# The end of the second mixture: DVE's order of the routed rows and the last two residuals

## What is computed

```python
x = x + tanh(g_ffn[1]) * ffn(layernorm(x))
# ffn, with 8 experts of width 176, two for each token, and a shared part of width 352:
shared = silu(x @ Ws_gate) * (x @ Ws_up) @ Ws_down
scores = softmax(x @ W_router);  topk_vals, topk_idx = top_k(scores, 2)
h = silu(einsum('td,edh->eth', x, We_gate)) * einsum('td,edh->eth', x, We_up)
routed = einsum('etd,te->td', einsum('eth,ehd->etd', h, We_down), combine)
return routed + shared
```

## Time and profile before

| | us |
|---|---|
| median of 3 runs | 683.2 |
| all runs | 682.86, 683.20, 689.97 |
| profiled execution | 675.47 |
| its span | 673.7 |

### The profile page before, as it was taken

One profiled execution on the slowest core, in us unless ns is written; L12 is line 12 of the kernel. 1 busy time (PEld: TensorE's weight loads), 2 busy tenths in 40 slices (PEclk: granted clock), 3 DMA queues, 4 the chain that ended last, 5 costly groups with the idle time before them and its releaser, 6 DMA issues. The chain is left out here.

```text
span 673.7 us, 16760 instructions
## 1 busy us (share of the span) xinstructions
PE 605.9 (90%) x5037; PEld 463.2 (69%) x5037; DVE 493.1 (73%) x999; ACT 404.8 (60%) x829; POOL 312.9 (46%) x430
## 2 busy tenths in 40 slices
PE   3688877999999968899999999999789799999995
PEld 2577765788888867455555555555578699999875
DVE  2877885778878796998989999995555634444756
ACT  3888883344434441688988988998545135555431
POOL 2455555023233556945765765752327334124254
PEclk9999995999999988799999999999969789999998
DMA  5434448400000014444444444440002325446344
GB/s 164 115 99 132 124 111 286 152 1 1 0 0 1 23 48 135 125 133 123 141 138 119 140 138 122 144 137 19 3 0 79 125 94 188 143 151 190 115 135 131
DMA packets 72601, 71.20 MB, mean 106 GB/s; under 512 B 12364, under 2 KB 68812, under 8 KB 72556
## 3 DMA queue, kind: packets, MB, share of 16 engines
q1 hardware_dynamic: 67324, 56.33, 28.2%
q0 software_dynamic: 5232, 14.29, 6.8%
HBM read 38.48 MB, written 31.36 MB: 104 GB/s over the span
## 5 line engine op out<-in xcount | busy, mean ns | idle before, releaser
L1426 DVE TENSOR_REDUCE a_smax<-a_s 128x2 f32<-128x512 f32 x256 | 164.3, 680 | 14.2 <-PE a_s L1354 9.1
L1245 ACT ACTIVATE a_prob<-a_st 128x512 f32<-128x512 f32 x256 | 141.9, 597 | 20.7 <-PE a_st L1344 19.5
L1344 PEld LDWEIGHTS a_st<-qop,kop 64*128 64x128 f32 x512 | 71.4, 188 | 59.9 <-DVE a_smax L1426 26.3
L1344 PE MATMUL a_st<-qop,kop 64*128 64x256 f32 x512 | 105.1, 317 | 2.9 <-DVE a_smax L1426 1.7
L1354 PE MATMUL a_s<-kop,qop 64*128 64x256 f32 x512 | 107.1, 319 | 0.0
L1306 PE MATMUL a_pv<-a_prob,a_vt 128*32 128x256 f32 x1024 | 82.5, 394 | 3.2 <-ACT a_pv_sb L1230 1.7
L823 POOL TENSOR_TENSOR f_hs_lo<-f_kept,f_hs_hi 128x512 fp32r<-128x512 f32 x32 | 41.2, 1319 | 86.7 <-ACT f_hs_hi L773 86.7
L1354 PEld LDWEIGHTS a_s<-kop,qop 64*128 64x128 f32 x512 | 73.4, 191 | 0.0
L1877 POOL DMA_INDIRECT sorted_rows<-m_xn,m_slot x32 | 33.5, 1048 | 48.7 <-PE m_gu L128 28.7
L126 PE MATMUL f_bank<-f_xt_hi,w_hi 128*128 128x512 f32 x128 | 51.6, 403 | 1.2 <-DVE w_raw L869 0.6
L127 PE MATMUL f_bank<-f_xt_lo,w_hi 128*128 128x512 f32 x128 | 51.0, 398 | 0.0
(11 more groups left out here) (267 smaller groups left out, 1685.6 us busy)
## 6 DMA issues: line engine op xcount, KB each, us to landing
qop<-qop_rows SPq DMA_DIRECT2D x64, 100.0 KB
kop<-kop_rows SPq DMA_DIRECT2D x64, 96.0 KB
sorted_rows<-x_all SPq DMA_DIRECT2D x2, 2944.0 KB, 15.4
qop<-sorted_rows SPq DMA_DIRECT2D x46, 128.0 KB, 2.4
expert_rows<-turned SPq DMA_DIRECT2D x46, 128.0 KB
kop_rows<-k_hi SPq DMA_DIRECT2D x32, 128.0 KB, 2.3
qop_rows<-q_hi POOLq DMA_DIRECT2D x30, 128.0 KB, 2.7
x_all<-in_x SPq DMA_DIRECT2D x4, 512.0 KB, 4.8
```

The lines of the kernel that those rows point to most:

```text
L1245: act.activation(prob[:, u % 8], st_ps[BANK[u]][:], ACT.Exp, scale=SCALE1).then_inc(prob_ready, 1)
L1344: st = pe.matmul(st_ps[BANK[u]][:, c * D:(c + 1) * D], lhsT=kop[t.slot][rows, u // 2, c * P:(c + 1) * P], rhs=qop[t.slot][rows, u // 2], s ...
L1426: dve.tensor_reduce(smax[:, v.slot, opposite(u)], s_ps[BANK[u]][:].rearrange("p (q n) -> p q n", q=2), AX_X, ALU.max).then_inc(smax_ready, 1)
```

## The change

DVE takes the same instructions in another order. routed(8) moves from n = 8 to n = 9. At n = 10 residual(2) comes first and routed(9) behind it; routed(10) is at n = 11. hidden_low(11) is followed by routed(11), routed(12), routed(13), then residual(3), then routed(14) and routed(15).

A tile's residual and routed additions write the same rows of `x_all`, so whichever is second waits for the first: residual(2) for routed_added 9 (tile 8), routed(9) for shared_added 12, residual(3) for routed_added 14 (tiles 12 and 13), routed(14) and routed(15) for shared_added 16. `routed` has a parameter for that. The last wait is for routed_added instead of shared_added. No other engine's program is changed.

```diff
-            def routed(t):
+            def routed(t, added=0):
 
                 dve.wait_ge(back_loaded[t], 16 * TOP)
+                if added:
+                    dve.wait_ge(shared_added, added)
                 for k in range(TOP):
                     if k:
                         dve.wait_ge(half_added, t + 1)
@@
-            arrivals = {HEAD + 2: (PT,), HEAD + 3: (PT + 1, PT + 2), HEAD + 4: (PT + 3, PT + 4), HEAD + 5: (PT + 5,)}
             for n in range(HEAD, N):
                 multiply(n)
                 if n > HEAD:
                     hidden_low(n - 1)
-                for t in arrivals.get(n, ()):
-                    routed(t)
+                if n == HEAD + 3:
+                    routed(PT)
                 if n == HEAD + 4:
-                    residual(2, PT + GT)
+                    residual(2, PT + 1)
+                    routed(PT + 1, 3 * GT)
+                if n == HEAD + 5:
+                    routed(PT + 2)
             hidden_low(N - 1)
+            for t in range(PT + 3, PT + 6):
+                routed(t)
+            residual(3, PT + 6)
             for t in range(PT + 6, TILES):
-                routed(t)
-            residual(3, TILES)
-            dve.wait_ge(shared_added, TILES)
+                routed(t, TILES)
+            dve.wait_ge(routed_added, TILES)
```

## The result

| | before | changed |
|---|---|---|
| median of 20 runs, us | 681.68 | 686.78 |
| lowest and highest, us | 678.71, 689.97 | 681.84, 691.02 |
| profiled execution, us | 675.47 | 686.84 |
| its span, us | 673.7 | 684.8 |

What follows compares the result with a forecast made beforehand. It took the end to be bound by gathers, then DVE's routed tiles and last residual. DVE's -1.07 us plus 0.4 for the last gather gave about -0.7 us: 682.5 us forecast, range 679.5 to 686.

Steps and rivals of the forecast that it cites:

- What bounds the kernel: End of kernel: gathers, then DVE's routed tiles and last residual; residual(2) behind routed(12)'s gather left TensorE idle 2.44 us.
- routed(8) one chunk later: DVE in chunk 9: one tile less ahead of multiply(10), where DVE idled 0.89 us anyway; worth nothing.
- residual(2) 3.4 us earlier: DVE, chunk 10: residual(2) starts at 658.08, ends at 659.74, and TensorE's 2.44 us idle time is gone.
- DVE up to hidden_low(11): DVE from residual(2) onward: multiply(11) 2.2 us earlier, hidden_low(11) at 663.0 instead of 665.60.
- TensorE's end: The last shared_down products at full clock: last result at 665.4, 3.8 us earlier, no longer setting the end.
- DVE behind hidden_low(11): DVE's tail: residual(3) at 666.57, DVE ends at 670.21, span 1.07 us shorter; two more tiles take back 1.84 us.
- The last gather: Gather ahead of routed(15): 1.0 us from the store and 0.3 from GpSimd later, landing at 669.6, costing DVE 0.4 us.
- The sum: Whole span: -1.07 + 0.4, about -0.7 us, giving 673.0 us.
- 1 and 2, the last gather: Rivals: gather lands at 670.2, span 673.6, -0.1 us, chance 0.22; or at 671.4, span 674.8, +1.1 us, chance 0.10.
- 3, the clock falls all the same: Rival at TensorE's end: last 24 matmuls take up to twice as long, span 674.15, +0.5 us; chance 0.06.
- 4, the reorder does nothing: Rival at residual(2): something else holds it; its only other wait, for shared_down(8), is over at 657.98; chance 0.02.
- The range: Measured time: mechanisms alone 682.0 to 684.3 us, widened by the spread of executions to 679.5 to 686.

Runs made afterwards that it cites:

- b1: The kernel before, unchanged, run again for a second trace; 679.63 us, ratio 0.9995 (0.9959 to 1.0031).
- b3: The kernel before, unchanged, a fourth trace in the batch of the changed kernel's third trace; 683.35 us.
- a4: The changed kernel as it is, fourth trace, without late signals; 670.47 us, ratio 0.9982 (0.9949 to 1.0015) to the kernel before.
- a3: The changed kernel as it is, third trace, with late signals; ratio 1.0046 (1.0011 to 1.0081) to the kernel before.
- e3: The changed kernel as it is, run again for a second trace, with late signals; ratio 1.0024 (0.9990 to 1.0059) to the kernel before.
- e1: The kernel before with only residual(2) moved ahead of routed(11) and routed(12), tail as before; ratio 0.9992 (0.9955 to 1.0029).
- e5: The kernel before with only residual(2) moved ahead of routed(11) and routed(12), repeated in a later batch; ratio 1.0009 (0.9976 to 1.0042).
- b2: The kernel before, unchanged, one look for a third trace; 680.51 us.
- e4: The changed kernel with routed(9) ahead of residual(2) instead of behind it; ratio 1.0043 (1.0011 to 1.0075) to the kernel before.
- g3: The changed kernel without GpSimd's 16 gathers of tiles 8 to 15 and DVE's waits for them, those tiles' results wrong; 676.47 us.

## Why the prediction was wrong

*What bounds the kernel.* The rows were read rightly, but they were those of an execution of 675.47 us, while the three runs shown beside it lay at 682.86 to 689.97. The prediction named this distance of 1.1% and took it for spread. It was a second bound, late signals of PE, that the earlier trace rows did not have. The traces b1 to b3 show what the end of before looks like with it: hidden_low(11) at 25.9 to 26.0 instead of 22.60.

*routed(8) one chunk later.* Costed at nothing, and nothing is seen of it in a4 or in the result: residual(2) finds DVE free in both.

*residual(2) 3.4 us earlier.* In a4 it starts at 15.02 where the forecast had 658.08 - 643.00 = 15.08, 3.46 us ahead of the earlier trace rows. PE has no gap over 0.2 us there, and shared_down(9) starts at 17.53, where 17.60 was expected. In the result's trace it starts at 18.89, not earlier at all; in a3's at 18.77 and in e3's at 15.89.

*DVE up to hidden_low(11), "at 663.0 instead of 665.60".* **This is the step that failed.** It rested on 0.10 us from the end of a matmul to whoever waits for it. That holds in a4 (hidden_low(11) at 19.91, forecast 20.0). With late signals the forecast 2.6 us earlier became 27.46 and 27.36 in two traces of the changed kernel and 25.86 in the third, against 25.86 to 26.00 in those of before: no gain, or 1.4 us lost. e1 and e3 show why an earlier residual does not help: hidden_high(11) waits for shared_down(9), whose signal comes 3.1 to 3.4 us late in b1 to b3 and 6.07 us late in e1 (in e3 it has no record, and hidden_high(11) starts 6.0 us behind the matmul's end), and then an earlier shared_down(9) is worth nothing. Before, part of the first late signal lay under the wait for routed(12)'s gather, as b3 shows. The extra 1.4 us of the result and of a3 stand with gate signals 8.21 and 8.09 us late, against 1.65 and 3.07 in b1 and b3. Whether the new order makes that signal later or two executions happened on a worse case is not settled: e3 has the same order and 1.60. Something speaks for both. Near 520 us, where all kernels have the same code, a gate signal is 5.8 us late in the traces of the result, a3, e5 and b3, and 2.7 to 2.8 in b1, b2, e1, e3 and e4, so there are worse executions. Of the four worse ones the three with residual(2) early have signals 8.1 to 9.6 us late at the end, and the one of before has 4.6 at most. That is one trace of before, too few to tell.

*TensorE's end.* In a4 the last matmul ends at 22.33; 665.4 - 643.00 = 22.4 was forecast.

*DVE behind hidden_low(11).* The prediction said that two more tiles there take 1.84 us of the gain back. They do so whether the gain came or not. From hidden_low(11) to the end before needs 7.9, 7.5 and 6.8 us (b1 to b3), the changed kernel 10.5, 9.8 and 9.5 us: 2.5 us more on average. The parts: residual(3) to DVE's end is 3.69 us where it was 1.65, since two tiles now follow it; residual(3) starts 0.8 us later behind hidden_low(11) on average; the tail is 0.3 us shorter. The 0.8 us is not the tiles' alone: in the result and in a3 residual(3) waits for TensorE behind its three tiles, 1.23 and 0.48 us; in e3, where it does not, it starts 3.57 us behind hidden_low(11), as forecast (666.57 - 663.0). So **the bill of this step stood, and the step that was to pay it failed**: 0 to 1.4 us lost up to hidden_low(11) and 2.5 us behind it agree with ratios of 1.0024 to 1.0062, 1.6 to 4.2 us. The forecast's prices of the tiles were right. In a4, residual(3) starts at 23.47 (forecast 23.57).

*The last gather.* DVE waits 0.37 us for it in a4, 0.4 was forecast, and DVE ends at 27.61, as 670.21 + 0.4 - 643.00. The transfer took 3.55 us, 0.7 more than the earlier trace rows, where I had 1.0. GpSimd's last four gathers took 1.36, 1.21, 1.00 and 1.13 us instead of 0.95, and the last one was issued at 23.03 where the earlier trace rows have 22.46, 0.57 later where I had 0.3. The Trainium skill (SBUF — State Buffer, Who interferes with whom) says that a VectorE instruction with two SBUF inputs and a GpSimd instruction that reads SBUF exclude each other. a4's rows agree: when these four gathers start, a DVE instruction with two SBUF inputs already runs (656.88, 658.39, 659.90 and 661.33) and has 0.53, 0.38, 0.18 and 0.31 us left, and the gather takes 0.41, 0.26, 0.05 and 0.18 us more than 0.95. In the result's trace the last four take 0.95 us: DVE is idle or in a residual, which reads PSUM, at the start of three, and the fourth, at 667.44, starts 0.02 us behind an addition of L1938 and is not held. No wait for a gather is left on DVE there, which was late enough by then.

*The sum.* Without late signals the stage is 29.80 us instead of 30.73, -0.93 us where -0.7 was forecast; -1.07 + 0.37 is the working, and 0.23 more came from a shorter tail (2.19 us instead of 2.42). The ratio, 0.9982 (0.9949 to 1.0015), holds both this and nothing.

*The rivals.* 1 and 2, the last gather: refuted, since it costs 0.37 us in a4 and nothing in the result. 3, the clock falls all the same: in a4 it does not, the windows show 1.00 up to 660.7. In the result's trace it does, but behind the late signals. Windows of it:

```profile
641.00:660.70 19.70, 19.20 (x103) 15.89 (x104) 9.57 (x19) 6.64 (x12) 9.31 (x9) 1.00 0.43 132
...
660.00:680.00 20.00, 12.03 (x62) 10.34 (x60) 10.44 (x22) 1.97 (x4) 7.52 (x8) 0.74 0.30 86
```

The columns are those of the earlier trace rows. PE is busy for 12.03 of 20 us, and the clock is 0.50 in part of it, from 668.2 us for 10.2 us. PE's first matmul behind its second wait there shows it:

```profile
673.44 0.58 PE L126 MATMUL m_y<-wds_hi,m_hs_hi 128*128 128x256 f32 x1 [3.84 <-DVE m_hs_lo L1913]
```

PE had idled for 2.91 us ahead of 667.37, for the residual(2) that the late signal held, and the wait here is for the hidden_low(11) that the next ones held. So the clock fell behind waits which the late signals explain. The low clock holds residual(3) for the 1.23 us of the timeline above. 4, the reorder does nothing because something else holds residual(2): the prediction gave it 0.02, with shared_down(8) "over at 657.98". This is nearest to what happened. shared_down(8) was over, and its signal was not there.

*The range.* 679.5 to 686 misses 686.78. It was made of the mechanisms seen in one trace and of the spread of three runs. A bound of 3 to 4 us for "the profiled execution is not of the runs' kind" was missing.

## What to carry to other kernels

Before a forecast rests on one trace, its time has to be held against the other runs of the kernel: one that lies 1.1% below all of them can lack a wait that the others have, and then its idle times say nothing about what an earlier start is worth. An edit that buys an earlier start on one engine with work moved to the end of another pays for certain and gains only if every signal on the way is prompt; so move the work only as far as something seen in all traces covers it. Where a timeline names "remote" or "issue" ahead of an instruction that waits for an engine, compare the producer's end with the consumer's start.

## What the runs showed of the hardware

*A gather on GpSimd is held by what DVE already runs*, where that has two SBUF inputs: by 0.05 to 0.41 us in a4's last four, each 0.12 or 0.13 us less than the DVE instruction had left. Those beside instructions that started behind the gather took 0.95 us (661.15 in the result's trace, with a hidden_low 0.08 us later).

*PE's signals can be late.* On the chips of the result and of three batches, semaphore updates carried by matmuls came 0.3 to 9.6 us behind the matmuls' recorded ends, 11 of 2,601 updates in the result's trace and 13 in e5's. No recorded one of DVE or ACT did; about 80 of theirs have no record in each of these traces. It is not an error of the recording: silu(11) started at 671.29, 0.02 us behind the recorded signal and 8.23 us behind the product's end. On the chips of three other batches no update was more than 0.3 us behind. Two chips differ here by more than this edit: before takes 679.09 to 682.48 us on the ones and 669.79 and 671.40 us (and once 675.04) on the others. The two kinds do not differ up to 500 us.

*They come with GpSimd's chains of indirect transfers*, and leaving the gathers out took them away at the end (g3, a single execution). Why a signal of PE is held, while the recorded ones of ACT and DVE are not, no run here shows; nor whether it is the transfers or GpSimd's part in them.

*The traces of such executions hold fewer records of semaphore updates*, about 9,550 instead of 10,650, and the loss begins near 500 us, where the late signals begin. Of the 2,601 updates of PE, DVE and ACT about 105 are missing in each, nearly all within 1 us of an indirect transfer's instruction, and in g3 none behind 640 us. So records go missing where signals come late. Both may have one cause, and the recording itself may have a part in it: it cannot have only shifted times on paper, as silu(11) shows, but whether the signals would be late without it was not tested.
